# Two transformer layers on one core: the lightning attention spread over all expert blocks, a third chunk buffer, and one swap on VectorE

## The chip, the cores and the metric

The kernel runs on one NeuronCore of a Trainium2 chip. Its engines are TensorE (PE, with PEld for its weight loads), VectorE (DVE), ScalarE (ACT), GpSimd (POOL) and SyncE (SP), which only issues DMAs here. The metric is the device time in microseconds of one execution. All times below are from runs on the chip or from one profiled execution.

## What is computed

Two layers on a [4, 512, 256] float32 input. Each layer adds an attention and a mixture of experts to its residual, both fed by the same normed input:

```
x  = x + attention_0(norm(x)) + experts_0(norm(x))
xn = norm(x)
x  = x + lightning_attention(xn) + experts_1(xn)
```

Layer 1 is what the change touches. Its lightning attention has 16 heads of 16 and works in chunks of 128 positions, four to a batch:

```
q, k, v  = silu(x Wq), silu(x Wk), silu(x Wv)
scores   = (q k^T) * D                       # D: decay by distance, causal
o        = scores v + (q S) * q_decay        # S: state at the chunk's start
S        = chunk_decay * S + (k * k_decay)^T v
o        = o * sigmoid(gate);  o = o * rsqrt(mean over each head of o*o + eps) * norm_w
out      = o Wo
```

Its experts are eight, two for each token: `y = (silu(x Wgate) * (x Wup)) Wdown`, weighted by the routed probabilities.

## The kernel before

Three stages run one after the other, with a barrier between: `layer0_front` (layer 0's experts and projections), `middle` (layer 0's softmax attention, and beside it, one batch behind, layer 1's norm, routing and the projections for its attention; to 640) and `layer1_main` (layer 1's experts and lightning attention; to the end).

**middle.** A hardware loop walks the batches. A pass has 16 slots (4 groups of heads x 4 tiles); in each, the attention's own work is done and then the steps that a table on each engine names for that slot work on the batch before. Four batches are done as two passes of the loop, one more pass behind it, and the last batch's steps alone. On DVE a slot holds four reductions of row maxima (L1305) and then the steps. Slot 13 holds `first_part` (L1408 to L1410: bf16 cast of k's transposed projection into `parts[0]`, which waits until the stores of q's parts have landed), `decay_k` (L1402: k times its decay into `kd`, read from PSUM `psX`), and `fold_next(3)` (L1367, L1369). On PE, slot 13 holds `turn_k` (L1633, writes `psX`) and slot 14 `project_gate` (L1624, writes `psX` again and so waits for `kd`), with this batch's row products for DVE's reductions (L1491) ahead of it and behind it in the slot, and slot 15 `project_v`. POOL's `rest` (L1207) waits for `first_part`. SP stores q's parts in slot 12 (L1131).

**layer1_main.** The 4096 pairs of token and expert are sorted into 39 blocks of 128 rows, each of one expert. A block goes through five kinds of PE steps: `turn` (transpose of the gathered rows, L1995), `gate` (L2008), `up` (L2016), `turn_h` (transpose of the hidden rows, L2025) and `down` (L2033). POOL gathers rows four blocks ahead (L1843) and scatters results (L1852), ACT has silu and the copies (L1872, L1878, L1884), DVE the product (L1908) and a copy (L1903).

The attention's 16 chunks have 12 light steps each. Steps 0 to 3: scores of a group of heads (PE L2047, DVE `weigh` L1913). Step 4: `own` (PE L2056, ACT copy L1890). Step 5: `updates` and `outputs` (PE L2066, L2080, L2083; DVE L1923). Step 6: `gate_out` (DVE L1929, state L1935, L1939, L1941, L1943), then the power -0.5 on POOL (L1858). Step 9: `normalise` (DVE L1947, L1951). Step 10: `turn_normed` (PE L2092, ACT L1894). Step 11: `project` (PE L2099) and the residual (DVE L1955). A chunk needs the one before it, through its PSUM tiles and its state.

The order of all this is one list that `main_order` writes and each engine walks, taking its own part of each entry. Each block from the second on gives five slots (190 in all), and `given < (len(steps) - tail) * used // slots` says how many light steps have been placed by then. With `tail = LSTEPS + LSTEPS // 2`, 174 of the 192 are placed in the slots, so that about one slot in twelve is empty, and 18 follow. Behind the last `down` stand chunk 14 from step 4 on and the whole of chunk 15. Among these, four `combine` entries (DVE L1977, 8 instructions each) merge the expert rows of one batch into the residual; they wait for that batch's attention and for SP's loads of the expert rows (L1828), and SP stores each batch behind its merge (L1833).

Inputs come through SP, in its own program order. `load_weights(e)` issues the three DMAs of an expert (L1783), `weights_loaded(e)` makes SP wait for them and raise `w_ready`, for which PE's `gate` waits by the block's expert. `load_chunk(n)` issues 16 DMAs: 12 stacks (L1796), v, kd, sg, qd (L1799 to L1802); buffers alternate between two, and chunk n waits until chunk n - 2 has passed `outputs` and its gate (`gated`).

## Time and profile before

| | us |
|---|---|
| median of 3 runs | 1027.42 |
| lowest and highest | 1027.22, 1032.19 |
| profiled execution, whole | 1029.67 |
| its span | 1027.9 |
| PE busy in the span | 853.7 (83%) |
| DVE, ACT, POOL busy | 573.2, 394.1, 310.5 |
| mean granted clock of PE | 0.896 |

Times in the profile count from the span's start. A group's busy time is the union of its instructions; a matmul's end is modelled and overlaps the next one's start, so costs of PE steps are read from start to start. PEclk is the clock granted to TensorE as a share of 2.4 GHz; its two levels are 1.0 (2.4 GHz) and 0.5 (1.2 GHz). "issue" is a wait for nothing that the profile shows.

### The profile page before, as it was taken

What the parts mean: (1) busy time and instruction counts of PE and PEld (TensorE: products, weight loads), DVE (VectorE), ACT (ScalarE), POOL (GpSimd) and SP (SyncE); (2) the same over time, 40 slices, a digit from 0 to 9 for tenths busy, and PEclk for the clock granted to TensorE, in tenths of its full rate; (3) what the DMA queues carried; (4) which work ended last, traced back from release to release, by engine and by line L of the source; (5) the groups of instructions that cost most, each with busy time, mean ns of one, the idle gap of its engine ahead of it and who ended that gap; (6) DMA issues with size and microseconds to landing.
All of it is one profiled execution on the core that took longest, in us unless ns stands there. A gap on an engine that the chain in (4) does not pass through costs nothing. (4 is left out here: it accounts for less than half of the span.)

```text
span 1027.9 us, 14864 instructions
## 1 busy us (share of the span) xinstructions
PE 853.7 (83%) x4544; PEld 490.8 (48%) x4544; DVE 573.2 (56%) x1269; ACT 394.1 (38%) x676; POOL 310.5 (30%) x250
## 2 busy tenths in 40 slices
PE   4999999668989979998888765099999899999963
PEld 4765665411224334343334544056666665666642
DVE  7746887177786776875855246024434333344337
ACT  2336666434554646465567222022222222222210
POOL 2034666352001510150133121113433333433231
PEclk9999999857989988988998765589999999999985
DMA  8414665372322324233321313946744334432254
GB/s 265 130 57 144 200 201 195 108 202 60 97 84 63 104 94 154 69 110 99 135 78 65 105 64 128 259 170 215 229 120 88 88 93 101 130 94 83 73 178 139
DMA packets 158353, 130.26 MB, mean 127 GB/s; under 512 B 64128, under 2 KB 139920, under 8 KB 158288
## 3 DMA queue, kind: packets, MB, share of 16 engines
q1 hardware_dynamic: 151136, 109.89, 35.7%
q0 software_dynamic: 7152, 19.54, 6.4%
q8 instruction: 37, 0.61, 0.2%
q14 instruction: 28, 0.23, 0.1%
HBM read 83.37 MB, written 46.01 MB: 126 GB/s over the span
## 5 line engine op out<-in xcount | busy, mean ns | idle before, releaser
L1305 DVE TENSOR_REDUCE b_negmax<-b_psM 128x1 f32<-128x512 f32 x256 | 163.2, 683 | 63.0 <-PE b_psM L1491 60.2
L1242 ACT ACTIVATE b_probs<-b_psE 128x512 f32<-128x512 f32 x256 | 138.8, 595 | 119.2 <-PE b_psE L1509 118.4
L1491 PE MATMUL b_psM<-b_kst,b_qst 96*128 96x512 bf16 x256 | 99.8, 435 | 30.2 <-DVE b_negmax L1305 14.0
L1509 PE MATMUL b_psE<-b_qst,b_kst 98*128 98x512 bf16 x256 | 89.6, 412 | 14.3 <-ACT b_probs L1242 9.6
L2008 PE MATMUL d_psG<-d_w,d_xT 128*128 x156 | 77.0, 616 | 24.4 <-SPq L1788 21.2
L1852 POOL DMA_INDIRECT scratch_ys<-d_y,put x39 | 40.2, 1030 | 149.1 <-ACT d_y L1884 147.9
L1518 PE MATMUL b_psV<-b_probs,b_vst 128*32 128x512 f32 x512 | 74.7, 658 | 2.5 <-ACT b_probs L1242 2.5
L1908 DVE TENSOR_TENSOR d_hidden<-d_hidden,d_psU 128x512 f32<-128x512 f32 x39 | 26.8, 687 | 86.8 <-PE d_psU L2016 86.8
L2033 PE MATMUL d_psY<-d_w,d_hidden 128*128 x312 | 75.0, 383 | 0.0
L2016 PE MATMUL d_psU<-d_w,d_xT 128*128 x156 | 75.0, 603 | 0.0
L1872 ACT ACTIVATE d_hidden<-d_psG 128x512 f32<-128x512 f32 x39 | 23.3, 597 | 127.0 <-PE d_psG L2008 127.0
L1509 PEld LDWEIGHTS b_psE<-b_qst,b_kst 98*128 98x128 bf16 x256 | 20.8, 99 | 105.7 <-issue 52.5
L1491 PEld LDWEIGHTS b_psM<-b_kst,b_qst 96*128 96x128 bf16 x256 | 24.3, 99 | 90.0 <-DVE b_negmax L1305 63.4
L1858 POOL TENSOR_TENSOR d_rs<-d_ss,d_neghalf 128x16 f32<-128x16 f32 x16 | 47.1, 2942 | 61.0 <-DVE d_ss L1943 60.9
L527 POOL DMA_INDIRECT a_xg<-scratch_xn,a_take x39 | 41.9, 1075 | 74.7 <-PE a_psXH L886 48.6
L2033 PEld LDWEIGHTS d_psY<-d_w,d_hidden 128*128 128x128 f32 x312 | 57.5, 190 | 13.5 <-issue 7.3
L1884 ACT ACTIVATE d_y<-d_psY 128x256 f32<-128x256 f32 x39 | 14.9, 383 | 123.4 <-PE d_psY L2033 123.4
L1913 DVE TENSOR_TENSOR d_probs<-d_ps,decay 128x512 f32<-128x512 f32 x64 | 43.4, 688 | 31.4 <-PE d_ps L2047 31.3
L1170 POOL TENSOR_TENSOR b_combined<-b_both 128x256 f32<-128x256 f32 x16 | 11.6, 725 | 160.6 <-DVE b_both L1349 160.6
L896 PE MATMUL a_psV<-a_w,a_xgT 128*128 x156 | 54.4, 472 | 4.1 <-issue 3.4
L1843 POOL DMA_INDIRECT d_xg<-scratch_xn,take x39 | 38.5, 988 | 56.7 <-PE d_psX L1995 29.3
L915 PE MATMUL a_psV<-a_w,a_hT 128*128 (+1 forms) x156 | 48.6, 410 | 4.1 <-ACT a_hT L610 4.1
(353 smaller groups left out, 1602.7 us busy)
## 6 DMA issues: line engine op xcount, KB each, us to landing
scratch_parts<-a_parts SPq DMA_DIRECT2D x12, 512.0 KB, 4.3
b_qst<-scratch_parts SPq DMA_DIRECT2D x96, 64.0 KB, 2.1
b_kst<-scratch_parts SPq DMA_DIRECT2D x96, 64.0 KB, 2.1
scratch_parts<-b_part SPq DMA_DIRECT2D x24, 256.0 KB, 3.4
d_qst<-scratch_parts SPq DMA_DIRECT2D x96, 64.0 KB, 2.6
d_kst<-scratch_parts SPq DMA_DIRECT2D x96, 64.0 KB, 2.9
scratch_ys<-a_y SPq DMA_DIRECT2D x39, 128.0 KB, 1.8
scratch_v<-a_xn SPq DMA_DIRECT2D x4, 1024.0 KB, 6.8
```

Source lines behind the costliest of these rows:

```text
L896: mm = nc.tensor.matmul(psM[:, b % 2, 0:2 * F0], xgT[b % 2][:, k, :], w[:, bass.ds(owner[b], 1), at:at + 2 * F0].rearrange("p a n -> p (a ...
L915: mm = nc.tensor.matmul(psY[:, 0:D], hTall[0:rows, b % 2, k, :], w[0:rows, bass.ds(owner[b], 1), at:at + D].rearrange("p a n -> p (a n)"), ...
L1242: nc.scalar.activation(probs[k % PSLOTS][:, h, :], psE[h % 2][:, :], ACT.Exp, scale=float(HD) ** -0.5).then_inc(scores_used[h % 2], 1)
L1305: nc.vector.tensor_reduce(negmax[i][:, t, h:h + 1], psM[:, h % 2, :], AX_X, ALU.max, negate=True).then_inc(rows_used[h % 2], 1)
L1491: nc.tensor.matmul(psM[:, h % 2, :], qst[g][0:STACK, h, t * P:(t + 1) * P], kst[g][0:STACK, h, :], start=True, stop=True).then_inc(rows_re ...
L1509: nc.tensor.matmul(psE[h % 2][:, :], kst[g][0:STACKM, h, k * P:(k + 1) * P], qst[g][0:STACKM, h, :], start=True, stop=True).then_inc(score ...
L1518: mm = nc.tensor.matmul(psV[VW * h:VW * (h + 1), :], vst[g][:, k, VW * h:VW * (h + 1)], probs[k % PSLOTS][:, h, :], start=k == 0, stop=k = ...
L1858: nc.gpsimd.tensor_tensor(rs[:, :], ss[:, :], neghalf[:, :], ALU.pow).then_inc(rs_done, 1)
L1913: nc.vector.tensor_tensor(probs[g][:, :], (ps1 if g % 2 else ps0)[:, :], decay[:, HG * g:HG * g + HG, :].rearrange("p h c -> p (h c)"), AL ...
L2008: mm = nc.tensor.matmul(psG[:, :], xT[b % 2][:, k, :], weights(b, GATE + k * H1, H1), start=k == 0, stop=k == KT - 1)
L2016: mm = nc.tensor.matmul(psU[:, :], xT[b % 2][:, k, :], weights(b, UP + k * H1, H1), start=k == 0, stop=k == KT - 1)
L2033: mm = nc.tensor.matmul(psY[:, 0:D], hT[b % 2][:, k, :], weights(b, DOWN + k * D, D), start=k == 0, stop=k == HT1 - 1)
```

## The change

1. `middle`, DVE, slot 13: `decay_k` now stands before `first_part`.
2. `main_order`: `tail = 2`. 190 steps go into the 190 slots, one to each, from the second block's first slot on; of chunk 15 only steps 8 to 11 stand behind the last `down` (`normalise`, `turn_normed`, `project` and the residual), and the four merges follow them.
3. `CSLOTS = 3` buffers for a chunk's inputs in place of 2, with `gated`, `chunk_in` and their counts to match.
4. SP's order: `load_chunk` is split into `load_stacks` and `load_rest`; SP waits for expert 0 (`weights_loaded(0)`) between the stacks and the rest of chunk 0; chunk 2 comes before experts 3 to 7; those are loaded one by one, each with a wait for the one before it behind its issue; chunks 3 to 15 follow.

```
-                               12: (route_weights, fold_next(2), place), 13: (first_part, decay_k, fold_next(3), spread_ids),
+                               12: (route_weights, fold_next(2), place), 13: (decay_k, first_part, fold_next(3), spread_ids),
...
+CSLOTS = 3
...
-    tail = LSTEPS + LSTEPS // 2
+    tail = 2
...
-    combine = {4: 0, 6: 1, NORMALISE: 2, PROJECT: 3}
-    for n, s in steps[given:]:
-        order.append(("light", n, s))
-        if n == CHUNKS - 1 and s in combine:
-            order.append(("combine", combine[s], 0))
+    order += [("light", n, s) for n, s in steps[given:]]
+    order += [("combine", b, 0) for b in range(BATCHES)]
...
-            def load_chunk(n):
-                s, b, t = n % 2, n // NC, slice(n % NC * CH, (n % NC + 1) * CH)
-                if n >= 2:
-                    sp.wait_ge(gated[s], n // 2)
+            def load_stacks(n):
+                s, b, t = n % CSLOTS, n // NC, slice(n % NC * CH, (n % NC + 1) * CH)
+                if n >= CSLOTS:
+                    sp.wait_ge(gated[s], n // CSLOTS)
                 for op, dst, parts in ((0, qst, Q_PARTS), (1, kst, K_PARTS)):
...
+            def load_rest(n):
...
+            def load_chunk(n):
+                load_stacks(n)
+                load_rest(n)
+
             sp.dma_start(ident[:, :], io["ident"]).then_inc(ident_in, 16)
             load_weights(0)
-            load_chunk(0)
+            load_stacks(0)
+            weights_loaded(0)
+            load_rest(0)
+            load_weights(1)
             for dst, src in ((sel[:, :], io["sel16"]), (blockmask[:, :], io["blockmask"]),
                              (normw[:, :], io["norm_w"].to_broadcast((P, D))),
                              (wo[:, :, :], io["Wo1"].rearrange("(k p) n -> p k n", p=P))):
                 sp.dma_start(dst, src).then_inc(consts_in, 16)
-            load_weights(1)
             load_chunk(1)
-            for e in range(2, E, 2):
+            weights_loaded(1)
+            load_weights(2)
+            load_chunk(2)
+            load_weights(3)
+            weights_loaded(2)
+            for e in range(4, E):
                 load_weights(e)
-                load_weights(e + 1)
-                weights_loaded(e - 2)
                 weights_loaded(e - 1)
-                load_chunk(e // 2 + 1)
-            weights_loaded(E - 2)
             weights_loaded(E - 1)
-            for n in range(E // 2 + 1, CHUNKS):
+            for n in range(CSLOTS, CHUNKS):
                 load_chunk(n)
```

Three places of the instruction order follow. The first is DVE in a pass of the loop of `middle`, behind the reductions of slot 13, as a difference (`-` before, `+` now):

```order
 L1305 TENSOR_REDUCE b_negmax<-b_psM 128x1
+L1401 REGISTER_ALU
+L1402 TENSOR_TENSOR b_kd<-b_psX,b_kdec 128x1024
 L1408 ISA
 L1409 ISA
 L1410 CAST b_part<-b_half 128x1024
-L1401 REGISTER_ALU
-L1402 TENSOR_TENSOR b_kd<-b_psX,b_kdec 128x1024
 L1367 ISA
 L1367 SCALAR_TENSOR_TENSOR xacc<-b_y,b_y_wts,xacc 128x256
```

`decay_k` (L1402) has passed `first_part` (L1410 and the two waits L1408, L1409).

The second is SP at the start of `layer1_main`, with the first rows behind the identity. Before:

```order
L1783 DMA d_w<-in_gate_dram 128x2x512
L1783 DMA d_w<-in_up_dram 128x2x512
L1783 DMA d_w<-in_down_dram 128x4x256
L1796 DMA d_qst<-scratch_parts 16x16x128 x6
L1796 DMA d_kst<-scratch_parts 16x16x128 x6
L1799 DMA d_v<-scratch_v 128x512
L1800 DMA d_kd<-scratch_kd 128x256
L1801 DMA d_sg<-scratch_sg 128x256
L1802 DMA d_qd<-scratch_qd 128x2x128
L1811 DMA d_sel<-in_sel_dram 128x64
L1811 DMA d_blockmask<-in_blockmask_dram 128x128
L1811 DMA d_normw<-in_norm_w_dram 128x256
```

Now, with the waits that stand ahead of a row (the semaphore of expert 0's loads bears an older name, `a_ln_xn`, in this listing):

```order
L1781 DMA d_w<-in_gate_dram 128x2x512
L1781 DMA d_w<-in_up_dram 128x2x512
L1781 DMA d_w<-in_down_dram 128x4x256
L1794 DMA d_qst<-scratch_parts 16x16x128 x6
L1794 DMA d_kst<-scratch_parts 16x16x128 x6
L1800 DMA d_v<-scratch_v 128x512 [waits a_ln_xn]
L1801 DMA d_kd<-scratch_kd 128x256
L1802 DMA d_sg<-scratch_sg 128x256
L1803 DMA d_qd<-scratch_qd 128x2x128
L1781 DMA d_w<-in_gate_dram 128x2x512
L1781 DMA d_w<-in_up_dram 128x2x512
L1781 DMA d_w<-in_down_dram 128x4x256
```

A wait has come between the stacks and v, and the four constants have gone behind the loads of expert 1. The second and later experts and chunks follow in the order of point 4.

The third is DVE from the last chunk's last weighing to the end. Before:

```order
L1913 TENSOR_TENSOR d_probs<-d_ps,decay 128x512 x4
L1977 SCALAR_TENSOR_TENSOR xacc<-d_w,wts,xacc 128x256 x8
L1929 TENSOR_TENSOR d_o<-d_ps,d_sg 128x256
L1939 TENSOR_TENSOR d_sq<-d_o 128x256
L1941 TENSOR_REDUCE d_ss<-d_sq 128x16
L1943 TENSOR_SCALAR d_ss<-d_ss 128x16
L1977 SCALAR_TENSOR_TENSOR xacc<-d_w,wts,xacc 128x256 x8
L1947 TENSOR_TENSOR d_o<-d_o,d_rs 128x256
L1951 TENSOR_TENSOR d_normed<-d_o,d_normw 128x256
L1977 SCALAR_TENSOR_TENSOR xacc<-d_w,wts,xacc 128x256 x8
L1955 TENSOR_TENSOR xacc<-d_ps,xacc 128x256
L1977 SCALAR_TENSOR_TENSOR xacc<-d_w,wts,xacc 128x256 x8
```

Now:

```order
L1921 TENSOR_TENSOR d_probs<-d_ps,decay 128x512 x2
L1916 TENSOR_TENSOR d_hidden<-d_hidden,d_psU 128x512
L1921 TENSOR_TENSOR d_probs<-d_ps,decay 128x512 x2
L1937 TENSOR_TENSOR d_o<-d_ps,d_sg 128x256
L1947 TENSOR_TENSOR d_sq<-d_o 128x256
L1949 TENSOR_REDUCE d_ss<-d_sq 128x16
L1951 TENSOR_SCALAR d_ss<-d_ss 128x16
L1955 TENSOR_TENSOR d_o<-d_o,d_rs 128x256
L1959 TENSOR_TENSOR d_normed<-d_o,d_normw 128x256
L1963 TENSOR_TENSOR xacc<-d_ps,xacc 128x256
L1985 SCALAR_TENSOR_TENSOR xacc<-d_w,wts,xacc 128x256 x32
```

The merges (32 instructions of L1985, before L1977) have moved behind the last residual, and the last two weighings stand on both sides of an expert product (L1916). POOL's last rows, before and now:

```order
L1858 TENSOR_TENSOR d_rs<-d_ss,d_neghalf 128x16
L1852 DMA scratch_ys<-d_y,put 9088x256 x2
L1858 TENSOR_TENSOR d_rs<-d_ss,d_neghalf 128x16
L1852 DMA scratch_ys<-d_y,put 9088x256 x3
L1858 TENSOR_TENSOR d_rs<-d_ss,d_neghalf 128x16 x2
```

```order
L1860 DMA scratch_ys<-d_y,put 9088x256 x3
L1866 TENSOR_TENSOR d_rs<-d_ss,d_neghalf 128x16
L1860 DMA scratch_ys<-d_y,put 9088x256 x2
L1866 TENSOR_TENSOR d_rs<-d_ss,d_neghalf 128x16
L1860 DMA scratch_ys<-d_y,put 9088x256
```

Two powers (L1858) stood behind the last scatter (L1852); now one (L1866) stands ahead of the last scatter (L1860) and none behind.

## Rows read from the trace of the kernel before

**Rows 1.** Windows, busy us of PE, PEld, DVE, ACT, POOL; granted clock; DMA share; GB/s
```profile
676.00:989.50 313.50, 299.34 (x1815) 197.50 (x1813) 124.46 (x259) 71.60 (x143) 113.05 (x85) 1.00 0.42 118
...
384.00:394.00 10.00, 10.00 (x44) 5.13 (x42) 3.60 (x6) 7.04 (x8) 0.00 (x0) 0.61 0.16 53
...
450.00:460.00 10.00, 9.92 (x40) 3.07 (x40) 7.99 (x28) 4.19 (x8) 3.54 (x2) 0.67 0.01 3
```

**Rows 2.** Timeline, 641 to 671: start us, us, engine, line, [idle before <-releaser]
```profile
645.17 4.34 SPq L1796 DMA_DIRECT2D d_kst<-scratch_parts  x6
...
649.04 0.42 DVE L1903 COPY d_xT<-d_psX 128x256 f32<-128x256 f32 x1 [2.05 <-PE d_psX L1995]
...
668.98 1.05 SPq L1783 DMA_DIRECT2D d_w<-in_down_dram  x1
670.24 1.22 PE L2008 MATMUL d_psG<-d_w,d_xT 128*128 x1 [21.24 <-SPq L1788]
```

**Rows 3.** Timeline, 985 to the span's end
```profile
989.61 0.38 ACT L1884 ACTIVATE d_y<-d_psY 128x256 f32<-128x256 f32 x1 [2.32 <-PE d_psY L2033]
...
992.73 7.56 SPq L1828 DMA_DIRECT2D d_w<-scratch_ys  x8
...
998.84 0.69 PE L2092 MATMUL d_ps<-d_ident,d_normed 128*128 128x128 f32 x2 [5.97 <-DVE d_normed L1951]
...
1021.14 3.38 DVE L1977 SCALAR_TENSOR_TENSOR xacc<-d_w,wts,xacc 128x256 f32<-128x256 f32 x8
```

**Rows 4.** Timeline, middle: DVE and PE around the store's wait, and L1624 at full clock
```profile
379.62 0.69 DVE L1410 CAST b_part<-b_half 128x1024 bf16<-128x1024 f32 x1 [3.78 <-DMA scratch_parts<-b_part]
...
381.60 3.75 PE L1624 MATMUL b_psX<-b_wg,b_lowT 16*128 16x256 f32 x8 [3.77 <-DVE b_kd L1402]
...
385.92 1.29 DVE L1305 TENSOR_REDUCE b_negmax<-b_psM 128x1 f32<-128x512 f32 x2 [1.40 <-PE b_psM L1491]
...
394.44 1.29 DVE L1305 TENSOR_REDUCE b_negmax<-b_psM 128x1 f32<-128x512 f32 x2 [5.44 <-PE b_psM L1491]
...
560.49 1.99 PE L1624 MATMUL b_psX<-b_wg,b_lowT 16*128 16x256 f32 x8
```

**Rows 5.** Source view of L1783, issues from 640 to 642 (expert 0)
```profile
DMA to landing us min/median/max: 3.7/4.5/6.6
```

**Rows 6.** Chain that ended last, on PE: start us, us, engine, tile, line
```profile
690.97 1.01 PE d_ps L2056 x32
...
693.02 0.85 PE d_ps L2083 x8
...
704.02 0.88 PE d_ps L2099 x4
...
714.93 0.63 PE d_ps L2080 x4
...
742.25 1.72 PE d_psU L2016 x4
```

**Rows 7.** Timeline, PE: first scores of chunk 0 and the step behind them
```profile
684.36 0.39 PE L2047 MATMUL d_ps<-d_qst,d_kst 96*128 96x128 bf16 x4
684.58 1.94 PE L2016 MATMUL d_psU<-d_w,d_xT 128*128 x4
```

**Rows 8.** Page, costliest groups: busy us, mean ns of one, idle before, releaser
```profile
L1858 POOL TENSOR_TENSOR d_rs<-d_ss,d_neghalf 128x16 f32<-128x16 f32 x16 | 47.1, 2942 | 61.0 <-DVE d_ss L1943 60.9
```

**Rows 9.** Timeline, PE: turn_normed of chunks 5 and 8
```profile
809.37 0.44 PE L2092 MATMUL d_ps<-d_ident,d_normed 128*128 128x128 f32 x2 [1.54 <-DVE d_normed L1951]
...
874.34 0.44 PE L2092 MATMUL d_ps<-d_ident,d_normed 128*128 128x128 f32 x2 [2.07 <-DVE d_normed L1951]
```

**Rows 10.** Waits, PE, 676 to 989.5: us in total, times, longest us
```profile
PE d_ps L2092 <- DVE d_normed L1951: 5.3, 5, 2.1
```

**Rows 11.** Source view of L1828, the loads of the expert rows
```profile
DMA to landing us min/median/max: 4.4/6.8/9.4
```

**Rows 12.** Page, slices of 25.7 us: DMA share in tenths
```profile
DMA  8414665372322324233321313946744334432254
```

More of the change, by code:

```diff
@@ L1733, in layer1_main @@
         normw, neghalf, wo = sb("normw", [P, D]), sb("neghalf", [P, HEADS]), sb("wo", [P, KT, D])
-        qst, kst = ([sb(f"{n}{s}", [STACK, HEADS, CH], BF16) for s in range(2)] for n in ("qst", "kst"))
-        v = [sb(f"v{s}", [P, HEADS, VW]) for s in range(2)]
-        kd, sg, qd = ([sb(f"{n}{s}", [P, D]) for s in range(2)] for n in ("kd", "sg", "qd"))
+        qst, kst = ([sb(f"{n}{s}", [STACK, HEADS, CH], BF16) for s in range(CSLOTS)] for n in ("qst", "kst"))
+        v = [sb(f"v{s}", [P, HEADS, VW]) for s in range(CSLOTS)]
+        kd, sg, qd = ([sb(f"{n}{s}", [P, D]) for s in range(CSLOTS)] for n in ("kd", "sg", "qd"))
         probs = [sb(f"probs{g}", [P, HG * CH]) for g in range(GROUPS)]
@@ L1751, in layer1_main @@
         neghalf_set = sem("neghalf")
-        chunk_in, gated = sems("chunk_in", 2), sems("gated", 2)
+        chunk_in, gated = sems("chunk_in", CSLOTS), sems("gated", CSLOTS)
         scores_ps, probs_done, probs_used = sems("scores_ps", GROUPS), sems("probs", GROUPS), sem("probs_used")
@@ L1798, in load_chunk @@
                                      .rearrange("k (h d) t -> d (k h) t", d=HD)).then_inc(chunk_in[s], 16)
+            def load_rest(n):
+                s, b, t = n % CSLOTS, n // NC, slice(n % NC * CH, (n % NC + 1) * CH)
                 sp.dma_start(v[s][:, :, :].rearrange("p h w -> p (h w)"), scratch["v1"][b, t, :]).then_inc(chunk_in[s], 16)
@@ L1926, in gate_out @@
             def gate_out(n):
-                s, c = n % 2, n % NC
+                s, c = n % CSLOTS, n % NC
                 dve.wait_ge(out_ps, n + 1)
@@ L1937, in gate_out @@
                     last.then_inc(state_done, 1)
-                dve.wait_ge(gated[s], n // 2 + 1)
+                dve.wait_ge(gated[s], n // CSLOTS + 1)
                 nc.vector.tensor_tensor(sq[:, :], o[:, :], o[:, :], ALU.mult).then_inc(squared, 1)
@@ L2037, in scores @@
             def scores(n, g):
-                s = n % 2
+                s = n % CSLOTS
                 if g == 0:
-                    pe.wait_ge(chunk_in[s], CHUNK_IN * (n // 2 + 1))
+                    pe.wait_ge(chunk_in[s], CHUNK_IN * (n // CSLOTS + 1))
                     pe.wait_ge(o_done, n)
@@ L2055, in own @@
                     for i in range(HG):
-                        mm = nc.tensor.matmul(ps0[VW * i:VW * (i + 1), g * CH:(g + 1) * CH], v[n % 2][:, HG * g + i, :],
+                        mm = nc.tensor.matmul(ps0[VW * i:VW * (i + 1), g * CH:(g + 1) * CH], v[n % CSLOTS][:, HG * g + i, :],
                                               probs[g][:, i * CH:(i + 1) * CH], start=True, stop=True,
@@ L2065, in updates @@
                 for k in range(KT):
-                    mm = nc.tensor.matmul(ps1[:, k * P:(k + 1) * P], kd[n % 2][:, k * P:(k + 1) * P],
-                                          v[n % 2][:, k * HH:(k + 1) * HH, 0:HD], start=True, stop=True, skip_group_check=True)
+                    mm = nc.tensor.matmul(ps1[:, k * P:(k + 1) * P], kd[n % CSLOTS][:, k * P:(k + 1) * P],
+                                          v[n % CSLOTS][:, k * HH:(k + 1) * HH, 0:HD], start=True, stop=True, skip_group_check=True)
                 mm.then_inc(update_ps, 1)
@@ L2079, in outputs @@
                     for k in range(KT):
-                        nc.tensor.matmul(ps0[:, k * P:(k + 1) * P], qd[n % 2][:, k * P:(k + 1) * P], state[:, k, :],
+                        nc.tensor.matmul(ps0[:, k * P:(k + 1) * P], qd[n % CSLOTS][:, k * P:(k + 1) * P], state[:, k, :],
                                          start=k == 0, stop=False, skip_group_check=True)
@@ L2096, in project @@
                 pe.wait_ge(normT_done, n + 1)
-                pe.wait_ge(gated[n % 2], n // 2 + 1)
+                pe.wait_ge(gated[n % CSLOTS], n // CSLOTS + 1)
                 for k in range(KT):
```

## Prediction

> **What bounds the kernel now.** I read the page's slices first, then the chain of waits, then the timelines of the places where the order changes. The diff touches two stages: `middle` (one swap on DVE) and `layer1_main`, which fills the last 388 of the 1027.9 us.
>
> In `layer1_main` PE is the bound. Between 676 and 989.5 it is busy 299.3 of 313.5 us at full clock, while DVE is busy 124 and the DMA queues 0.42 [rows 1]. So here PE work costs its own length, and only 14.2 us of idle time are there to be won or added to. Around this stretch lie two holes. At the front PE stands idle for 21.24 us before its first expert matmul at 670.24, and the releaser is SP's queue: SP has issued the first weights long before, but says so (`w_ready`) only behind its issues for chunks 0 and 1, the constants and three more experts, whose last issue starts at 668.98 and takes 1.05 [rows 2]. At the back PE ends the last expert block at 989.6, and 38.3 us pass until the span's end, in which the rest of chunk 14 and all of chunk 15 run alone, each step waiting for the one before, with the merges threaded between [rows 3].
>
> In `middle` the bound changes from slot to slot. At 377.8 PE comes to `project_gate`, which waits for `decay_k`. DVE has that behind `first_part`, and `first_part` waits for a store: DVE idles 3.78 us, PE 3.77 us [rows 4].
>
> **The change part by part.**
>
> *Start of layer1_main.* SP now issues the identity, three loads of expert 0 and the twelve stacks of chunk 0, and then waits for expert 0. The stacks' last issue ends at 645.17 + 4.34 = 649.5. The last of the three weight loads was issued at 641.4 and landed at most 6.6 us later, at 648.0 [rows 2, 5], so the new wait is over when SP comes to it. The first input is turned and copied by 647; the second copy starts at 649.04 [rows 2], and only block 1 needs it. PE's first matmul moves from 670.24 to 649.7: **20.5 us won**. Everything issued behind the wait is no later than before: v, kd, sg and qd follow at 649.5 as now, chunk 1 still follows the constants and expert 1. Chunk 0 was first read 14.1 us behind the first matmul, at 684.36 [rows 7], and is now read one short step sooner: at about 663.5, 12 us after its last issue. Expert 1 is announced at about 666, after chunk 1, and the first block that could need it is block 4, at about 677 by the pace of the blocks. If the loads queue worse than now, some 2 us go.
>
> *The later loads.* Expert 4 to 7 are loaded one by one, each behind a wait for the one before, at a landing of 3.7 to 6.6 us [rows 5]; chunk 3 is queued behind them on SP. By these landings SP is through at about 700, chunk 3 is in at 711. A chunk takes twelve slots: 2.4 blocks of 5.9 us, 4.6 of its own and a wait, some 19.5 in all, so chunk 3 is read at 722. The third buffer lets a chunk be loaded about 49 us ahead; with two it was 30, and PE waits for no chunk today [rows 10]. I cost both at nothing; the cover is those 11 us.
>
> *The spread.* Before, 174 light steps are spread over 190 slots and 18 are left; now it is one step to each slot and 2 are left. Moved in front of the last expert block's end are all PE instructions of chunk 14 from `own` on and those of chunk 15 up to `outputs`. By start-to-start times: `own` 2 x 1.01, L2083 2 x 0.85, L2080 2 x 0.63, `project` 0.88 [rows 6]; scores 4 x 0.22 (684.36 to 684.58) [rows 7]; update and turn some 0.65 at the same rate per matmul. That is **7.4 us** of PE time at full clock where PE is the bound.
>
> The second price of the spread is waiting. From a chunk's `outputs` to its `turn_normed` there are now always five slots, one of each kind: three groups of 1.72 [rows 6] and two turns, 5.9 us of expert work. Before, a skipped slot made it up to 7.6 for some chunks. In between run four DVE steps, POOL's power of 2.94 us [rows 8] and two DVE steps, about 5.4 to 6.0 us with nothing queued ahead. What it costs depends on the kind of slot of `outputs`. After `turn_h`, the gating stands behind the product of the block's up step on DVE: 2.07 us at 874.34. After `up`, the power stands behind a scatter on POOL: 1.54 at 809.37 [rows 9]. After gate or turn none showed, after `down` 0.3. Now three chunks each are of the kinds `turn_h` and `up`, and three of `down`; with 0.6 more where the state is updated between, that is 6.8 + 4.6 + 2.1 = 13.5 us, against 5.3 in all today [rows 10]: **8.2 us lost**. The other short waits of PE (scores behind the residual, `own` behind the last weighing) grow with the density by 1.4. In the last block, `own` follows the scores directly (0.9), `outputs` waits for the heads' copy (0.75), `down` 38 for the hidden copy (0.75), and the projection of chunk 14 for its copy (0.7): 3.1. Together **4.5 us lost**. Bounds for all waiting: 2 us (if the kinds cost what the mean chunk costs now) to 20.
>
> *The end.* Let D be the end of the last `down` on PE. Its copy is ready at D + 0.4, and now the scatter stands on POOL behind the power of chunk 15, which is free 1.1 us later than the scatter started before. SP's loads of the expert rows start at D + 4.2 instead of D + 3.1 [rows 3]. The first two loads need at least 4.4 and 0.4 us more [rows 11]: D + 9.0. Chunk 15's normalise, turn, projection and residual are done by D + 5, under these loads. Then four merges of 3.38 each follow with nothing between: D + 22.6; the last load lands at about D + 17.3, before the fourth merge wants it. From the last merge to the span's end it is 3.4 as before: D + 26.0 against 38.3, **12.3 us won**. Bounds: 9 (if each merge waits 1 us for its rows) to 13.5.
>
> *middle.* With `decay_k` first, it runs from 375.85 to 377.1 in DVE's hole and PE's `project_gate` starts at 377.8 instead of 381.60. DVE still waits for the store until 379.62, then casts (0.69), folds, and reduces some 1.2 us earlier than before, since `decay_k`, which stood between 380.3 and 381.5, is done. PE's next row products want only these reductions (382.7), so the pair that DVE reduced at 385.92 comes at about 383.3: 2.6 us earlier. From there to the next reduction at 394.44 PE is busy throughout, and DVE waits 5.44 us for it [rows 4]; PE works at 0.61 of full clock there [rows 1]. `project_gate` at full clock takes 1.99 where it now takes 3.75 [rows 4]. If PE keeps its clock, that stretch shrinks by another 2. It occurs in two passes of the loop; in the third batch DVE casts in a hole before PE's turn, and behind the last all inputs are ready: nothing there, except that POOL's subtraction starts 1.8 later, under cover. Two passes at 4.3: **8.6 us won**. Bounds 2 (only DVE's order) and 11.
>
> The clock decides between 2.6 and 4.3 a pass. PE's pause shrinks from 3.77 to some 3 us, and has 2 us of matmuls ahead of it. I take the higher, since `project_gate` ran at half clock right behind the pause (3.75) and at full clock in the third batch, which has no such pause (1.99) [rows 4]. Against it: in the row of 450 to 460 PE is busy 9.92 of 10 us at a granted 0.67 [rows 1], so a busy PE alone does not hold the clock. The Trainium skill ("TensorE: Matmul & The Clock Gate", the section on the HAM clock gate) says that the low clock is the idle state and that activity releases it. By that rule the half clock behind the shorter pause goes and the two passes give 8.6; by the row it may stay and they give 5.2. This trace does not support the rule whole.
>
> **Sum:** 20.5 + 8.6 - 7.4 - 8.2 - 4.5 + 12.3 = 21.3 us. The profiled execution took 1029.67 us around a span of 1027.9, 2.25 more than the median of the three runs, 1027.42. Its span would become 1006.6; the median **1006.1 us**.
>
> **Rivals.**
>
> *Waits stay as rare as now, the clock holds (faster still).* The chain after `outputs` costs PE only what the mean chunk pays now, 5.3 / 14 = 0.4 us [rows 10]: 7 us less, and the front's own order may win 1 more: 998. For: two chunks with exactly five slots paid nothing. Against: those that paid most also had five.
>
> *Loads give back part of the front.* The DMA queues stand at 9 tenths in the slice from 642 to 668 [rows 12], and PE will now work inside that time, so its gathers and the first chunks compete; or SP, waiting before each of the experts 4 to 7, brings chunk 3 late. If chunk 3 comes 10 us after 722, the gain is 11: 1016.
>
> *The chain paces PE (slower).* If in each of 15 chunks the power waited for a scatter that itself waits for its block's last copy, the mean wait would be 3 us and not 0.9: 31.5 us more, 1037.6. It decides from a mean of 2.3 us, 1.4 more than I take. For: with nothing beside it the wait is 5.97 [rows 3]. Against: 2.07 is the worst of fourteen under cover, and the kinds repeat.
>
> *The front does not move.* If the wait for expert 0 were served late, or another input were the last, PE would start at 670 still: 1026.6, no change. Against: its inputs are copied by 649.5.
>
> **Chances.** A gain of 13 to 27 by the mechanism above: 0.73. Rare waits, 998 and below: 0.10. Loads, 1014 to 1020: 0.11. No change: 0.03. Slower: 0.03. A measurement of this kernel tells 0.5%, 5 us, from no change. Faster 0.94, same 0.03, slower 0.03. The range takes the middle at 2.6 a pass and the waiting at 10 us above the sum to one side (1016), and the rare waits to the other (998).
>
> **What the profile will show if this is right.** PE's first `d_psG` at about 641 (649.7 less the middle's 8.6) with a wait under 1 us for SP; L1402 ahead of L1410 and PE's wait for `b_kd` gone, with `project_gate` at about 2 us; waits for `d_normed` summing to 13 us in about nine chunks; one power between the last `down` and the last scatter; four merges in a row without gaps, and 26 us from the last `down` to the end. I am wrong if PE waits for a chunk or for SP after its first block, if DVE idles between merges, if DVE's hole at the store only moves and PE meets it again in the next slot, or if the waits for `d_normed` sum to over 35 us.

## The result and the profile after

| | before | after |
|---|---|---|
| median, same chip | 1027.40 us (6 runs, 1026.72 to 1032.19) | 1018.88 us (6 runs, 1017.07 to 1022.64) |
| ratio | | 0.991, 95% interval 0.989 to 0.993 |
| profiled execution, its span | 1029.67, 1027.9 us | 1019.28, 1017.5 us |
| the same pair on a second chip (run e5) | 1029.95 us | 1016.23 us, ratio 0.987 (0.984 to 0.990) |

The change is faster by 8.5 us on the first chip and by 13.7 on the second. 1006.1 was predicted, with a range from 998 to 1016; both medians lie above it. The sign is right, the size is not.

**Front.** The timeline of the changed kernel, PE and SP around the first blocks (start us, us, engine, line):

```profile
639.18 0.35 SPq L1810 DMA_DIRECT2D d_ident<-in_ident_dram  x1
...
648.00 0.42 DVE L1911 COPY d_xT<-d_psX 128x256 f32<-128x256 f32 x1 [1.88 <-PE d_psX L2003]
...
648.29 0.87 SPq L1800 DMA_DIRECT2D d_v<-scratch_v  x1
...
648.38 3.60 PE L2016 MATMUL d_psG<-d_w,d_xT 128*128 x4 [0.41 <-SPq L1786]
```

This answers to [rows 2]. The first expert matmul comes 9.20 us behind the stage's first load (648.38 - 639.18); before it was 30.24 (670.24 - 640.00). That is 21.0 us. SP's stage starts at 639.18 and not at 640.00. That 0.8 us is not `middle` alone: the first reductions of row maxima (L1305) already start at 209.05 and not at 211.94, though all code ahead of them is the same. In the fourteen traces of this study, over several chips, they start between 209.05 and 213.42. So in this pair `middle` itself is 2.1 us longer than before.

**The long stretch.** Waits of PE from the first gate to the last `down` (us in total, times, longest):

```profile
PE d_ps L2100 <- DVE d_normed L1959: 13.1, 10, 2.5
PE d_ps L2064 <- DVE d_probs L1921: 4.1, 7, 0.9
PE d_psG L2016 <- issue: 2.6, 5, 0.6
PE d_ps L2055 <- DVE xacc L1963: 1.7, 6, 0.4
...
PE d_psG L2016 <- SPq L1786: 0.4, 1, 0.4
```

No wait for a chunk. The first line was 5.3 us in 5 [rows 10]. The 10 waits, from PE's timeline, are of the three kinds that the prediction priced:

```profile
699.03 0.44 PE L2100 MATMUL d_ps<-d_ident,d_normed 128*128 128x128 f32 x2 [1.55 <-DVE d_normed L1959]
...
741.92 0.44 PE L2100 MATMUL d_ps<-d_ident,d_normed 128*128 128x128 f32 x2 [2.08 <-DVE d_normed L1959]
...
846.21 0.69 PE L2100 MATMUL d_ps<-d_ident,d_normed 128*128 128x128 f32 x2 [2.07 <-DVE d_normed L1959]
846.69 3.35 PE L2024 MATMUL d_psU<-d_w,d_xT 128*128 x4
...
868.94 0.44 PE L2100 MATMUL d_ps<-d_ident,d_normed 128*128 128x128 f32 x2 [0.70 <-DVE d_normed L1959]
```

1.55 is chunk 1, whose `outputs` stand behind an `up`; 2.08 and 2.07 are chunks 3 and 8, behind a `turn_h`; 0.70 is chunk 9, behind a `down`. The longest, 2.47, is chunk 13 (952.98), behind a `turn_h` too. From the first gate to the last output copy the stretch was 319.4 us (670.24 to 989.61) and is now 341.9 (648.38 to 990.24): 22.5 more.

**End.** Timeline behind the last `down`:

```profile
988.66 2.93 POOL L1866 TENSOR_TENSOR d_rs<-d_ss,d_neghalf 128x16 f32<-128x16 f32 x1 [4.46 <-DVE d_ss L1951]
...
990.24 0.38 ACT L1892 ACTIVATE d_y<-d_psY 128x256 f32<-128x256 f32 x1 [2.17 <-PE d_psY L2041]
...
991.79 1.16 POOL L1860 DMA_INDIRECT scratch_ys<-d_y,put  x1 [0.20 <-issue]
...
994.44 7.94 SPq L1836 DMA_DIRECT2D d_w<-scratch_ys  x8
...
1000.88 13.26 DVE L1985 SCALAR_TENSOR_TENSOR xacc<-d_w,wts,xacc 128x256 f32<-128x256 f32 x32 [4.86 <-DMA d_w<-scratch_ys]
```

This answers to [rows 3]. From 990.2 to the span's end it is 27.3 us instead of 38.3: 11.0 won. So the two spans differ by 21.0 + 0.8 - 22.5 + 11.0 = 10.3; they read 10.4. The sum of the prediction was 21.3.

**middle.** Waits of PE between 250 and 638, the kernel before:

```profile
PE b_psM L1491 <- DVE b_negmax L1305: 8.8, 30, 1.2
PE b_psX L1624 <- DVE b_kd L1402: 7.4, 2, 3.8
```

and the changed kernel:

```profile
PE b_psM L1491 <- DVE b_negmax L1305: 17.8, 32, 5.3
```

The wait for `b_kd` is gone, as forecast, and the next wait has grown by 9.0 us: 16.2 in all before, 17.8 now. The timeline of the first pass after shows how:

```profile
372.82 1.22 DVE L1402 TENSOR_TENSOR b_kd<-b_psX,b_kdec 128x1024 f32<-128x1024 f32 x1
...
374.81 1.99 PE L1624 MATMUL b_psX<-b_wg,b_lowT 16*128 16x256 f32 x8
...
378.05 0.69 DVE L1410 CAST b_part<-b_half 128x1024 bf16<-128x1024 f32 x1 [4.02 <-DMA scratch_parts<-b_part]
...
378.66 0.48 DVE L1367 SCALAR_TENSOR_TENSOR xacc<-b_y,b_y_wts,xacc 128x256 f32 x1
...
378.82 2.29 POOL L1207 TENSOR_TENSOR b_half<-b_half,b_part 128x1024 f32<-128x1024 f32 x1 [15.78 <-DVE b_part L1410]
...
379.17 2.22 DVE L1369 SCALAR_TENSOR_TENSOR xacc<-b_y,b_y_wts,xacc 128x256 f32 x1
381.32 2.67 DVE L1305 TENSOR_REDUCE b_negmax<-b_psM 128x1 f32<-128x512 f32 x4
...
382.06 1.21 PE L1491 MATMUL b_psM<-b_kst,b_qst 96*128 96x512 bf16 x2 [5.25 <-DVE b_negmax L1305]
```

`project_gate` runs at full clock, 1.99 us instead of 3.75 [rows 4]. Then PE stands for 5.25 us, because the reductions that free its PSUM banks are queued on DVE behind the cast that waits for the store, and behind two folds, of which the second took 2.22 us. The half clock is still there: windows of the changed kernel (busy PE, PEld, DVE, ACT, POOL; granted clock; DMA share; GB/s)

```profile
379.00:388.00 9.00, 5.95 (x18) 1.77 (x19) 6.73 (x9) 3.18 (x6) 2.12 (x1) 0.50 0.17 58
```

In the last batch, whose steps run alone, the swap loses time. DVE's and POOL's rows there, before:

```profile
621.45 2.12 POOL L1207 TENSOR_TENSOR b_half<-b_half,b_part 128x1024 f32<-128x1024 f32 x1 [5.80 <-DVE b_part L1410]
...
624.96 0.55 DVE L297 TENSOR_SCALAR b_routes_ids<-b_routes_inblk,b_routes_p 128x1280 bf16<-128x1280 bf16 x1
```

and in the changed kernel:

```profile
621.02 3.31 POOL L1207 TENSOR_TENSOR b_half<-b_half,b_part 128x1024 f32<-128x1024 f32 x1 [7.38 <-DVE b_part L1410]
...
622.38 2.31 DVE L297 TENSOR_SCALAR b_routes_ids<-b_routes_inblk,b_routes_p 128x1280 bf16<-128x1280 bf16 x1
```

POOL's subtraction now meets other rows of DVE's routing. It takes 3.31 us instead of 2.12, and DVE's L294 and L297 together 3.8 instead of 3.1. From the first of `decay_k` and `first_part` to DVE's last routing step (L346) it is 14.9 us in the four traces without the swap and 15.6 in the ten with it. SP's next stage starts 4.5 us behind L346 in each of `before`, the change, e5 and e6, so these 0.7 us are paid in full.

### The profile page after: what moved, and what is told of

Read it like the earlier page. It is cut to its first block and busy times, and to the rows that moved or that the text cites. A ratio compares the mean times of both kernels' runs of the same rounds, so it can differ in the third digit from the quotient of the medians.

```text
span 1017.5 us, 14864 instructions
## 1 busy us (share of the span) xinstructions
PE 848.2 (83%) x4544; PEld 485.5 (48%) x4544; DVE 576.6 (57%) x1269; ACT 394.9 (39%) x676; POOL 312.2 (31%) x250
## 5 line engine op out<-in xcount | busy, mean ns | idle before, releaser
L1305 DVE TENSOR_REDUCE b_negmax<-b_psM 128x1 f32<-128x512 f32 x256 | 163.1, 682 | 62.7 <-PE b_psM L1491 59.6
L1491 PE MATMUL b_psM<-b_kst,b_qst 96*128 96x512 bf16 x256 | 100.4, 437 | 39.2 <-DVE b_negmax L1305 23.0
L1860 POOL DMA_INDIRECT scratch_ys<-d_y,put x39 | 40.3, 1033 | 157.9 <-ACT d_y L1892 156.5
L1491 PEld LDWEIGHTS b_psM<-b_kst,b_qst 96*128 96x128 bf16 x256 | 24.6, 100 | 98.9 <-DVE b_negmax L1305 73.5
L1916 DVE TENSOR_TENSOR d_hidden<-d_hidden,d_psU 128x512 f32<-128x512 f32 x39 | 26.8, 687 | 67.8 <-PE d_psU L2024 67.8
L1892 ACT ACTIVATE d_y<-d_psY 128x256 f32<-128x256 f32 x39 | 14.9, 383 | 127.1 <-PE d_psY L2041 127.1
L1866 POOL TENSOR_TENSOR d_rs<-d_ss,d_neghalf 128x16 f32<-128x16 f32 x16 | 46.9, 2934 | 51.2 <-DVE d_ss L1951 51.2
L1851 POOL DMA_INDIRECT d_xg<-scratch_xn,take x39 | 38.5, 988 | 33.6 <-POOLq L76 15.6
```

The lines of the kernel that those rows point to most:

```text
L1305: nc.vector.tensor_reduce(negmax[i][:, t, h:h + 1], psM[:, h % 2, :], AX_X, ALU.max, negate=True).then_inc(rows_used[h % 2], 1)
L1491: nc.tensor.matmul(psM[:, h % 2, :], qst[g][0:STACK, h, t * P:(t + 1) * P], kst[g][0:STACK, h, :], start=True, stop=True).then_inc(rows_re ...
L1866: nc.gpsimd.tensor_tensor(rs[:, :], ss[:, :], neghalf[:, :], ALU.pow).then_inc(rs_done, 1)
```

## The experiments

Each group of runs used one chip, with the kernel before beside it; only ratios compare across chips. Groups: e1 to e4 (before: 1049.23 us, 19 runs), e5 to e8 (1029.95, 11 runs), e9 to e12 (1028.25, 11 runs).

| run | median us | ratio to before, 95% interval |
|---|---|---|
| e1 swap only | 1043.73 | 0.995 (0.992 to 0.998) |
| e2 front only | 1028.96 | 0.978 (0.974 to 0.981) |
| e3 spread only | 1059.55 | 1.009 (1.005 to 1.012) |
| e4 change, folds first | 1027.09 | 0.979 (0.975 to 0.983) |
| e5 the change | 1016.23 | 0.987 (0.984 to 0.990) |
| e6 change without swap | 1021.79 | 0.993 (0.991 to 0.995) |
| e7 change, gating direct | 1001.75 | 0.973 (0.971 to 0.975) |
| e8 change, 12 steps left | 1018.13 | 0.988 (0.986 to 0.991) |
| e9 e7 with folds first | 997.71 | 0.970 (0.968 to 0.972) |
| e10 e9 with first_part late | 997.23 | 0.970 (0.968 to 0.973) |
| e11 e10 with 8 steps left | 991.89 | 0.966 (0.963 to 0.968) |
| e12 e10 with 12 steps left | 992.63 | 0.966 (0.964 to 0.968) |

### e1 and e6: the swap alone, and the change without it

```diff
-  13: (first_part, decay_k, fold_next(3), spread_ids),
+  13: (decay_k, first_part, fold_next(3), spread_ids),
```

e1 puts this line into the kernel before; e6 takes it out of the changed one.

> The kernel before with nothing but the swap of decay_k and first_part in the vector engine's list for slot 13. Theory A (what the trace after suggests): the swap does not shorten middle at all. PE only trades its wait for decay_k against a wait of about 5 us for the reductions behind first_part, and the middle stage loses 1 to 2 us, because first_part and with it the last subtraction come later: 1028 to 1029.5 us against 1027.4. Theory B (the term of my sum): 8.6 us won, 1018.8; if the clock stays low, 5.2 won, 1022.2.

> The changed kernel with decay_k and first_part in the old order. Theory A (the swap only moves PE's wait; its sign is set by where the clock's drops fall): within 3 us of the changed kernel, either side. Theory B (my sum): 5 to 9 us slower than the changed kernel.

Measured: e1 is 0.5% faster than before (5.1 us of 1049 by the ratio, 5.5 between the medians); e6 is 5.6 us slower than e5 on the same chip. (For e5 itself 0.985 was expected if the three parts add up, and 0.991 if the swap gives nothing; it measured 0.987, 0.984 to 0.990.) From the traces of the first pair I had come to expect no gain, or a loss: that expectation fell in e1, and its "within 3 us" in e6. e6 lies at the low edge of what my sum gave. PE's timeline of e6 and of e5 in the first pass:

```profile
381.45 3.44 PE L1624 MATMUL b_psX<-b_wg,b_lowT 16*128 16x256 f32 x8 [3.82 <-DVE b_kd L1402]
```

```profile
375.87 1.99 PE L1624 MATMUL b_psX<-b_wg,b_lowT 16*128 16x256 f32 x8
...
382.73 1.21 PE L1491 MATMUL b_psM<-b_kst,b_qst 96*128 96x512 bf16 x2 [4.87 <-DVE b_negmax L1305]
```

So the swap is worth about 5.4 us by the medians, not 8.6, with wide bounds (2.3 to 8.0 us by e1's interval). In every trace with the swap and the old place of the folds PE's wait moved on instead of going. Where the 5.4 us come from, the traces do not show. In the pair e5 and e6 the next stage's first load comes at 636.50 and 641.61, but 1.7 of these 5.1 us stand ahead of slot 13 (PE's L1633 at 371.38 and 373.06). Of the other 3.4 us, the granted clock can be a part: 0.86 behind that point in e5, 0.85 in e6.

### e2: the front alone

The diff is the change less its swap, with `tail` and the `combine` table of the kernel before.

> The change with its swap undone and with the old order of layer1_main (18 light steps behind the last block, merges threaded between them); what is left of the change is the note behind expert 0, the split of chunk 0 and the third chunk buffer. Theory A: the front gives the 21.0 us that the two traces show between the first identity load and the first gate matmul, and nothing of it is given back: 1006.4 us, 12 us faster than the whole change. Theory B: the loads or the density behind the earlier start take part of it back (the first chunks late, PE waiting for chunks): 1010 or more.

Measured: 0.978 of before, 23.5 us by the ratio (19.5 to 27.5), 20.3 between the medians; theory A held, nothing is given back. PE's waits from the first gate to the last `down` in e2:

```profile
PE d_ps L2103 <- DVE d_normed L1962: 5.3, 5, 2.1
...
PE d_psG L2019 <- SPq L1789: 1.2, 1, 1.2
```

No chunk is waited for, and the waits for `d_normed` are those of [rows 10] again. This part alone is faster than the whole change, by ratios on two chips (0.978 against 0.987).

### e3: the spread alone

```diff
-    tail = LSTEPS + LSTEPS // 2
+    tail = 2
...
-    combine = {4: 0, 6: 1, NORMALISE: 2, PROJECT: 3}
...
+    order += [("light", n, s) for n, s in steps[given:]]
+    order += [("combine", b, 0) for b in range(BATCHES)]
```

> The kernel before with two light steps left behind the last block and the four merges behind them; two chunk buffers, old order of the loads, no swap. Theory A: the spread costs what the traces show, 22.5 us between the first gate and the last down, and wins 11.0 behind it, net 11.5 lost: 1038.9 us. Of the 22.5, 1.7 is a drop of the clock at 846 us that may not come again, so 1037 to 1039. Theory B (my sum: 20.1 lost, 12.3 won): 1035.2. Rival: with two buffers only, PE waits for chunks as well: over 1041.

Measured: 1.009 of before, 9.0 us slower (4.9 to 13.0); both theories lie inside. The waits of PE in e3 from 686 on are those of the whole change:

```profile
PE d_psG L2005 <- SPq L1785: 20.7, 1, 20.7
PE d_ps L2089 <- DVE d_normed L1948: 13.3, 11, 2.5
```

No wait for a chunk, with two buffers: at this density the third buffer is not needed. (It was not tried whether two are enough with the early front.) The stretch from the first gate to the last output copy is 344.2 us in e3, against 323.4 in e1 and 321.4 in e2 on the same chip, and from there to the span's end it is 26.8 against 39.2 and 39.2. So the spread costs some 22 (20.8 to 22.8) and wins 12.4.

### e7: gating and power directly behind outputs

The order of PE is left as it is. Light step 6, which has no work on PE, is emitted with step 5; its slot stays empty.

```diff
-                order.append(("light", *steps[given]))
+                n, s = steps[given]
+                if s != 6:
+                    order.append(("light", n, s))
+                if s == 5:
+                    order.append(("light", n, 6))
```

> The changed kernel with light step 6 (the gating on DVE and the power on POOL) put directly behind outputs and not one slot later; PE's order is unchanged, turn_normed still comes five slots behind outputs. Theory A (as in my prediction: after turn_h the gating stands behind the product of the up step, after up the power stands behind a scatter): the waits of PE for d_normed fall from 13.1 us to under 3, 10 us won, about 0.990 of the changed kernel. Theory B (the chain of four DVE steps, the power and two DVE steps is itself as long as the five slots): the waits stay above 8 us and less than 4 us are won.

Measured: 14.5 us faster than e5 on the same chip, where theory A had 10. All waits of PE that sum to over 1 us in the stretch:

```profile
PE d_ps L2068 <- DVE d_probs L1925: 4.1, 7, 0.9
PE d_psG L2020 <- issue: 2.6, 5, 0.6
PE d_ps L2059 <- DVE xacc L1967: 1.7, 6, 0.4
PE d_ps L2092 <- issue: 1.3, 3, 0.8
PE d_ps L2111 <- ACT d_normT L1906: 1.3, 4, 0.5
PE d_psG L2020 <- SPq L1790: 1.1, 1, 1.1
```

The waits for `d_normed` fell from 13.1 us to 0.7, the others stand to a tenth. Theory A: what stood in the way was only the order on DVE and POOL, since the chain itself fits into five slots. The stretch is 328.3 us against 342.1 in e5, 13.9 less: 12.4 of waits, and 1.5 that fit the drop of the clock that e5 had behind its longest wait (below); this last part is argued. So the waiting term is shown by removing it. How it divides between DVE and POOL is not, since e7 moves both.

### e8 and e12: twelve steps left

e8: `tail = LSTEPS`, with the merges put in by

```diff
+    combine = {8: (0,), TURN: (1, 2), PROJECT: (3,)}
```

e12 stands on e10 (below) and has `{4: (0,), 8: (1,), 9: (2,), PROJECT: (3,)}`, for chunk 15 only.

> The changed kernel with twelve light steps left instead of two, all of chunk 15, run behind the last block under the loads of the expert rows and the merges (one merge before its normalise, two before its residual, one behind). Theory A: 3.4 us of PE work (scores, own, outputs of chunk 15) and the 3.1 us of waits in the last block leave the stretch where PE is the bound; behind the last down the end grows from 27.3 to 28 to 29 us: 5 us won. Theory B: chunk 15's chain is the longer one behind the last down (18.2 us in the trace before, from its scores to its residual, plus a merge and the stores) and each merge waits for it: 3 us lost.

> As e10, with twelve light steps left (all of chunk 15) and the first merge ahead of its gating, not behind it: in the run with twelve steps before, the first merge stood behind a gating at 997.5, 15.5 us behind the last down, while its rows were there some 6 us earlier, and the end grew by 7.8 us against 7.2 won. Theory A (that order was the fault): the end is 29 us, 2.6 more than with two steps, the stretch 7 us shorter: 4 us faster than e10. Theory B (chunk 15's own chain sets the end): within 1.5 us of e10 or slower.

Measured: e8 is 1.9 us slower than e5, which is inside the noise (1014.0 to 1021.6 against 1013.3 to 1020.9); the 5 us of its theory A did not come. e12 is 4.6 faster than e10. In e8 the stretch is 7.2 us shorter than in e5 (335.0 against 342.1), and the end 7.8 longer (34.9 against 27.1). DVE in e8, whose last output copy starts at 981.98:

```profile
997.52 0.42 DVE L1939 TENSOR_TENSOR d_o<-d_ps,d_sg 128x256 f32<-128x256 f32 x1 [5.66 <-PE d_ps L2093]
...
998.98 3.38 DVE L1987 SCALAR_TENSOR_TENSOR xacc<-d_w,wts,xacc 128x256 f32<-128x256 f32 x8
```

DVE stands idle for 5.66 us with a merge behind it in the queue. In e12, last output copy at 958.23, the first merge is ahead of the gating:

```profile
968.48 3.38 DVE L1999 SCALAR_TENSOR_TENSOR xacc<-d_w,wts,xacc 128x256 f32<-128x256 f32 x8 [1.56 <-DMA d_w<-scratch_ys]
...
972.58 0.42 DVE L1951 TENSOR_TENSOR d_o<-d_ps,d_sg 128x256 f32<-128x256 f32 x1 [0.72 <-PE d_ps L2105]
```

Its end is 30.6 us against 26.7 in e10, and its stretch 318.4 against 327.6: 5.4 net by the trace. Theory A of e12 held. Theory A of e8 failed, and the likely reason is my own placing of the merges; e12 differs from e8 in the gating and in `middle` as well, but those do not touch chunk 15 behind the last `down`.

### e4, e9 and e10: what PE waits for in middle

e4 is the changed kernel, and e9 is e7, with the folds in DVE's hole:

```diff
-  13: (decay_k, first_part, fold_next(3), spread_ids),
+  13: (decay_k, fold_next(3), first_part, spread_ids),
```

> The changed kernel with fold_next(3) moved ahead of first_part in slot 13, so that the two folds run in DVE's idle time of about 4 us before the store has landed instead of behind it. Theory A: what PE waits for behind project_gate is the reductions, and they stand behind first_part and 2.7 us of folds (0.48 and 2.22); PE's wait of 5.25 us in the first pass falls to about 2.6, the same in the second: 5.4 us won, 1013.5 against 1018.9. Theory B: PE is held there by something else (the clock, the store), or DVE's work beside POOL's subtraction is slowed whatever it is: within 1 us of 1018.9.

> The changed kernel with the gating put directly behind outputs (14.5 us faster than the change on the last chip, 0.973 of before) and fold_next(3) ahead of first_part. Theory A (what holds PE behind project_gate is the reductions, and the folds stand ahead of them): PE's wait of 4.4 to 5.3 us in slot 14 of the first pass halves, 5 us won over the kernel with the gating alone: 0.968 of before. Theory B: no gain from the folds, 0.973.

e10 moves `first_part` behind the reductions too, in all batches but the last:

```diff
-  13: (decay_k, fold_next(3), first_part, spread_ids),
-  14: (second_part, spread_rows),
+  13: (decay_k, fold_next(3), first_part_last, spread_ids),
+  14: (first_part_loop, second_part, spread_rows),
```

> As the run before it in this list, and first_part moved from slot 13 to slot 14, behind decay_k, the folds and one reduction, in all batches but the last. Theory A (the wait of my sum: DVE stands in first_part for the store and PE behind it for the reductions, so the swap only moved the wait): now PE finds its reductions done, the wait of 2.4 us and more behind project_gate is gone in the loop's passes, and what remains of my 8.6 us for middle comes back: 3 to 5 us faster than the run before it. Theory B: second_part, which must wait for POOL's subtraction of 2.1 us behind first_part, now holds DVE and PE the same time: within 1.5 us of it.

Measured: e4 0.979 against 0.987 of the change, e9 0.970 against 0.973 of e7, both across chips and so less sure: 3 to 8 us for the folds, e9 between its two theories (0.968 and 0.973). PE in the first pass of e9:

```profile
377.87 1.99 PE L1624 MATMUL b_psX<-b_wg,b_lowT 16*128 16x256 f32 x8
...
381.72 1.21 PE L1491 MATMUL b_psM<-b_kst,b_qst 96*128 96x512 bf16 x2 [1.86 <-DVE b_negmax L1305]
```

The wait is 1.86 us instead of 4.87 to 5.25. In e10 it is gone, and the sum of this wait over `middle` is near where it stood before the change:

```profile
PE b_psM L1499 <- DVE b_negmax L1305: 9.8, 34, 1.2
```

That is 8.0 us less than the 17.8 of the change, and the `b_kd` wait has not come back. The waits are thus explained. The time of e10 is that of e9 all the same, within 0.5 us: theory B of e10 by the time, though PE did not wait in the place that it names. From the first `b_v` to the second it is 88.6 us in e10 against 89.1 in e9, and to the third 85.9 against 84.2. These last 1.7 us are the clock's: the same 224 matmuls keep PE busy for 43.96 us at a granted 0.87 in e10 (511.5 to 563.4), and for 42.25 at 0.90 in e9 (514.0 to 564.2). And the half clock behind `project_gate` did not go with the wait: in e10 the window from 381.1 to 387.7 stands at 0.50, with PE busy for 6.24 of its 6.60 us.

### e11: eight steps left

`tail = 8`, merges at `{8: (0,), 9: (1,), PROJECT: (2, 3)}`.

> As e10, with eight light steps left (chunk 15 from own on), merges threaded: the first two ahead of its normalise and its turn, two behind its residual. Theory A: own and outputs of chunk 15 (2.5 us) and the last block's waits for them (2.4 us) leave the PE-bound stretch, the end grows by 1 to 2 us (26.4 to 28): 3 us faster than e10. Theory B: as with twelve steps, the end grows by as much as the stretch shrinks: within 1.5 us of e10 or slower.

Measured: 5.3 us faster than e10, 0.966 of before, the fastest kernel of the study together with e12 (within 1 us). The stretch is 5.0 shorter (322.6 against 327.6), the end the same, 26.7. The scatter no longer stands behind a power on POOL: it starts 0.7 us behind the last output copy and not 1.6. That this pays for chunk 15's gating behind the last `down` is argued.

Not tried was the early front with the swap, the folds and the direct gating, but with 18 steps left as before. So it is open whether any denser spread is worth its cost.

## Why the prediction was wrong

The traces give 10.3 us where the sum has 21.3. Of the 11.0 missing, `middle` with what stands ahead of it is 7.8, the spread 2.4 and the end 1.3; the front gave 0.5 more than forecast.

**The front: right.** "20.5 us won"; 21.0 in the traces, 20.3 us between the medians of e2 and before (23.5 by the ratio). The landing, the order of the inputs, and the cover for the later loads all held. The rival that loads give part of it back fell with e2.

**middle: the step that failed.** "Two passes at 4.3: 8.6 us won." e1 and e6 give 5.1 to 5.6; the first pair of traces only 0.8, and that with a lead of 2.9 that stood ahead of `middle`. Three sub-steps were wrong. First, "the pair that DVE reduced at 385.92 comes at about 383.3": I took away `decay_k` from in front of the reductions, but the store's wait, the cast and both folds stayed in front of them, and one fold, now started beside POOL's subtraction, took 2.22 us instead of 0.49. PE's L1491 behind `project_gate` started at 385.27 before and at 382.06 after, when everything in the changed execution already ran 2.9 us earlier for reasons ahead of the swap (`b_negmax` reductions at 373.07 and 370.13 in the two). Nothing but 0.3 us was won there. I named this as a way to be wrong ("if DVE's hole at the store only moves and PE meets it again in the next slot") and gave it no price. Second, "I take the higher": `project_gate` took its 1.99 us, but PE did not keep its clock behind it (the window from 379.00 above). The pause was 5.25 us, not some 3; that the pause is the cause is not shown, since e10 has half clock in this place without it. Third, behind the last batch "nothing there": the swap costs 0.7 us there, as POOL's later subtraction is not under cover but slows DVE's routing steps. The lower value, 2.6 a pass and 5.2 in all, is near what e1 and e6 measured, but this is luck: its 2.6 is the earlier pair of reductions, of which the trace shows 0.3.

**The spread: right in kind, some 2 us short.** Between first gate and last `down` I had 7.4 + 8.2 + 4.5 = 20.1; the traces show 22.5. The waits for `d_normed` went from 5.3 to 13.1, 7.8 against 8.2 forecast, with each kind at its price (1.5, 2.1, 0.7). All other waits grew from 8.1 to 12.6, just the 4.5 forecast. The rest, 10.2, is PE work, where I had 7.4: that term was mis-sized. 1.4 of it is an `up` step at half clock (3.35 us at 846.69 instead of some 1.95). Some 0.6 to 1.0 can only be argued: an expert step of four matmuls that has a light step beside it reads 1.94 to 1.98 us in the timeline, without one 1.88, and ten more light steps with work on PE now stand in the stretch. At least the last half microsecond stays open, and rather more, since PE also had 0.7 us less to pay at the start of the stretch, where the low clock ended 3.3 us behind the first gate (at 651.7) and 4.8 before (at 675.1).

**The end: right, 1.3 short.** "12.3 us won"; 11.0, and 12.4 in e3. SP's loads start at D + 4.2 as forecast, the four merges take 13.3 without a gap, and from the last one to the end it is 3.4. But the first merge starts at D + 10.6 and not D + 9.0. The loads of the expert rows took at least 6.7 us to land here, where [rows 11] has 4.4. From the view of their source line after:

```profile
DMA to landing us min/median/max: 6.7/7.8/8.6
```

The DMA engines are busy for 0.96 of the time from 995.5 to 1004.5, about as before (0.94 from 993.5 to 1003.0), so this does not tell the two apart. In e3 the shortest landing is 4.5 us and the first merge starts at D + 10.2 all the same, so the shortest landing is not what the merge waits for; which load it was stays open.

**The sum.** With the measured parts, the front's 20.3 to 21.0, the swap's 5.4 and the spread's 9.0 to 11.5 give a gain of 14.2 to 17.4. The second chip shows 13.7. The first shows 8.5. What separates those two is settled only in part. The two intervals touch (0.989 to 0.993, 0.984 to 0.990). And the two traces of the changed kernel, which run the same code, differ mainly in `middle`: from L1633 in slot 13 to the next stage's first load it is 268.86 us on the first chip and 265.12 in e5, with PE busy for 215.56 us at a granted 0.84 and for 210.19 at 0.86. So these 3.7 us go with the clock and not with the code. In the first pair the reductions were already 2.9 apart ahead of `middle`. Of that lead the changed kernel lost 1.2 us in the slots 13 to 15 of its third batch (DVE's copies to `b_outT` at 550.77 and 571.89 before, 548.93 and 571.25 after) and 1.4 between the last `b_v` and the next stage's first load, of which 0.7 is the swap's loss in the last batch; in between it won some back. To divide the rest between the swap and the clock would take many traces of one chip.

The forecast net of the spread alone was 7.8 us of loss, and this was inside the sum from the start: front and swap without the spread would have been the better kernel by the prediction's own numbers, as e2 shows for the front.

## What to carry to other kernels

Before an operation is moved out of a wait, list what else stands behind that wait on the same engine, and who needs it next: the wait must be passed by all of it, or it comes back one step later under another name. Spreading work into a stretch where PE is the bound costs its full length; it pays only for what then overlaps behind the stretch, and a few steps left (8 here) overlap as well as two. A step that has work on several engines need not stand at one place for all of them: the gating moved by one slot on DVE and POOL alone gave 14.5 us, more than the whole change. And one trace of each kernel cannot price a swap of a few microseconds here: the first reductions of `middle`, behind code that is the same in all fourteen traces, started up to 4.4 us apart.

## What the hardware showed that I had not expected

A drop of TensorE to 1.2 GHz can stand behind a wait of only 2 us in a stretch that is else at full clock. Behind the wait of 2.07 us at 846.21 the changed kernel shows

```profile
846.30:849.60 3.30, 3.30 (x6) 1.72 (x7) 0.00 (x0) 0.38 (x1) 1.28 (x2) 0.50 0.80 197
850.00:853.00 3.00, 3.00 (x21) 2.59 (x20) 1.22 (x3) 0.33 (x1) 0.00 (x0) 1.00 0.35 116
```

and e5 the same behind 2.47 us at 949.06, e8 behind 2.47 at 721.27 and 2.46 at 962.75. Other waits of the changed kernel, of 2.08 and 2.47 us, had no such drop (741.92, 952.98), so these waits do not force it. In e7 and e9 to e12, where no wait of the stretch is over 1.1 us, there was none. The Trainium skill ("TensorE: Matmul & The Clock Gate", the section on the HAM clock gate) says that activity releases the low clock. The rows do not contradict it: PE was busy 3.30 of 3.30 us while the clock was low, and the clock rose behind that. But they show a drop where PE had only paused for 2.07 us.

DVE and POOL hold each other up. The fold at 379.17 took 2.22 us and ended 0.3 us behind POOL's subtraction (378.82 + 2.29); alone it takes 0.48. The Trainium skill ("SBUF — State Buffer", "Who interferes with whom") says that a DVE instruction with two SBUF inputs contends with a GpSimd one that reads SBUF, and it calls the shared ports an exclusive lock. The trace agrees, at 471.35 and 558.54 as well (2.23 us each). In the kernel before, `decay_k` stood between `first_part` and the folds, and there the first fold took 1.43 us and the second 0.49.
